# Modulation's second layer as three split products from the third tile on

## The reference

```python
ctx  = causal_ema(x, tau_ctx)
wg   = sigmoid(concat(x, ctx) @ Wg.T + bg)
gated = x * wg
h1   = gelu(x @ Wn1.T + bn1)                 # 128 channels
mod  = 0.5 + sigmoid(h1 @ Wn2.T + bn2)       # 4 numbers per token
traces = [causal_ema(gated * mod[..., d], tau[d]) for d in range(4)]
temporal = sum_d(traces[d] * softmax(blend)[d])
out  = (gelu(x @ Wsoma.T + bsoma) * sigmoid(temporal @ Wtemp.T + btemp)) @ Wout.T   # then a layer norm
```

## Time and profile before

| what | us |
|---|---|
| median of three runs | 1363.86 |
| profiled execution, its own time | 1364.18 |
| its span | 1362.5 |
| TensorE busy | 1353.7 |
| VectorE busy | 779.8 |
| ScalarE busy | 481.2 |
| GpSimd busy | 134.6 |

### The profile page before, as it was taken

The page is one execution under the profiler, slowest core; times in us unless marked ns, Lnnn a source line. Parts: engine busy times, 40 slices in busy tenths (PEclk is TensorE's granted clock), DMA queues, the critical chain, the costliest instruction groups (busy, mean ns, idle before and its releaser), DMA issues.

```text
span 1362.5 us, 15161 instructions
## 1 busy us (share of the span) xinstructions
PE 1353.7 (99%) x5912; PEld 1105.8 (81%) x5912; DVE 779.8 (57%) x1035; ACT 481.2 (35%) x799; POOL 134.6 (10%) x170
## 2 busy tenths in 40 slices
PE   9999999999999999999999999999999999999998
PEld 7888888888888888888887887878787878787877
DVE  4335243333252332342221586999999989898994
ACT  5444233332242432332321223243424342424253
POOL 5000100000100000100000221012101220032000
PEclk9999999999999999999999999999999999999999
DMA  5523433502532412631322945621232123212101
GB/s 134 140 70 116 125 107 123 155 16 101 139 121 80 154 43 87 165 109 46 101 78 86 210 158 193 163 89 62 93 124 94 62 94 124 93 63 93 47 16 62
DMA packets 68375, 140.89 MB, mean 103 GB/s; under 512 B 7328, under 2 KB 19616, under 8 KB 64336
## 3 DMA queue, kind: packets, MB, share of 16 engines
q1 hardware_dynamic: 61360, 116.71, 27.8%
q0 software_dynamic: 6944, 23.23, 5.7%
HBM read 86.85 MB, written 53.05 MB: 103 GB/s over the span
## 4 chain that ended last, share of the span: by engine, by line
PE 93%; DVE 4%; DMA 1%; issue 1%; ACT 0%; POOL 0%; SPq 0%; DVEq 0%; POOLq 0%
PE bank L990 31%; PE bank L991 31%; PE bank L992 31%; DVE drive L1423 1%; DMA x_slot<-x2hl_dram 1%; DVE drive L1408 1%; PE bank L1057 1%; DVE temporal L1433 0%; PE bank L1165 0%; DVE temporal L1423 0%; DMA mod_t<-mod_dram 0%; DMA x_raw<-in_x 0%; DVE spikes_lo L1267 0%; ACT temporal L840 0%; DVE gated L1392 0%
## 5 line engine op out<-in xcount | busy, mean ns | idle before, releaser
L1267 DVE TENSOR_TENSOR h_hl<-bank,h_hl 128x512 fp32r<-128x512 f32 x128 | 88.7, 693 | 465.9 <-ACT h_hl L862 465.9
L990 PE MATMUL bank<-x_hl,wa 128*128 128x512 f32 x512 | 199.7, 390 | 0.9 <-DVE x_hl L1267 0.9
L992 PE MATMUL bank<-x_hl,wa 128*128 128x512 f32 x512 | 199.2, 389 | 0.0
L991 PE MATMUL bank<-x_hl,wa 128*128 128x512 f32 x512 | 199.2, 389 | 0.0
L992 PE MATMUL bank<-h_hl,wa 128*128 128x512 f32 x512 | 199.2, 389 | 0.0
L990 PE MATMUL bank<-h_hl,wa 128*128 128x512 f32 x512 | 199.2, 389 | 0.0
L991 PE MATMUL bank<-h_hl,wa 128*128 128x512 f32 x512 | 199.2, 389 | 0.0
L858 ACT ACTIVATE bank<-bank,small_sb 128x512 f32<-128x512 f32 x128 | 84.2, 658 | 212.2 <-PE bank L992 212.1
L862 ACT ACTIVATE h_hl<-bank 128x512 fp32r<-128x512 f32 x128 | 76.7, 599 | 228.5 <-PE bank L992 228.0
L990 PEld LDWEIGHTS bank<-x_hl,wa 128*128 128x128 f32 x512 | 96.1, 188 | 23.1 <-DVE x_hl L1267 1.7
L992 PEld LDWEIGHTS bank<-x_hl,wa 128*128 128x128 f32 x512 | 96.2, 188 | 20.0
(11 more groups left out here) (163 smaller groups left out, 2315.9 us busy)
## 6 DMA issues: line engine op xcount, KB each, us to landing
x_slot<-x2hl_dram SPq DMA_DIRECT2D x32, 513.0 KB, 4.7
x2hl_dram<-x_hl POOLq DMA_DIRECT2D x28, 512.0 KB, 9.1
stage<-in_l_w SPq DMA_DIRECT2D x32, 256.0 KB, 3.1
x_dram<-x_raw SPq DMA_DIRECT2D x8, 1024.0 KB, 5.6
xt<-x_dram SPq DMA_DIRECT2D x8, 1024.0 KB, 5.7
mod_t<-mod_dram POOLq DMA_DIRECT2D x8, 1024.0 KB, 5.0
x_raw<-in_x SPq DMA_DIRECT2D x7, 1024.0 KB, 9.3
out<-y_sb SPq DMA_DIRECT2D x28, 256.0 KB, 2.3
```

Source lines behind the costliest of these rows:

```text
L990: eng.matmul(ps, w_hi, x_hi, start=first, stop=False)
L991: eng.matmul(ps, w_hi, x_lo, start=False, stop=False)
L992: return eng.matmul(ps, w_lo, x_hi, start=False, stop=final)
L1267: return eng.tensor_tensor(lo, raw, hi.bitcast(F32), ALU.subtract)
```

## The change

`mo(i)` for i > 1 becomes a `split_product` with 128x128 weights: the 4 columns of wn2 are put, high and low part, into a block of zeros `wn2_hl`. `h1` is split into `h1_hi` (ScalarE, at the place of `sumsq`) and `h1_lo` (VectorE, in place of `h1`). `mo(i)` is issued after 12 matmuls of `gate(i, 0)` and not after 6. On ScalarE `temporal_hi(r-1, 3)` goes ahead of `h1_of(r)`. On VectorE `h1_low(r)` is the first step of round r, behind `temporal_low(r-1, 2)`. `mo(0)` and `mo(1)` stay.

```diff
+        h1_lo = place("h1_lo", 4, [TOK], F32R)
+        h1_hi = place("h1_hi", 30, [TOK], F32R)
+        wn2_hl = place("wn2_hl", 127, [2, P], F32R)
# GpSimd
             for i in range(NT):
                 if i % HALVES == 0:
                     last_columns(i)
+                if i == 0:
+                    on.wait_ge(s_fc2, UNITS)
+                    eng.memset(wn2_hl[:, :, :].bitcast(F32), 0.0).then_inc(s_wn2, 1)
                 if i + 1 < NT:
                     modulation(i + 1)
# ScalarE
+            def h1_hi_of(i):
+                on.wait_ge(s_h1, i + 1)
+                on.wait_ge(s_pe["SS"], i - 1)
+                eng.activation(h1_hi[:, :], h1[:, :], ACT.Copy).then_inc(s_h1hi, 1)
# in o_of(i, m), m == 0, i > 0
                         on.wait_ge(s_pe["SS"], i)
+                        on.wait_ge(s_pe["MO"], min(i + 2, NT))
# ahead of soma_of(1, 0)
+            on.wait_ge(s_wn2, 1)
+            eng.activation(wn2_hl[:, 0, 0:TAUS], wn2_sb, ACT.Copy).then_inc(s_wn2, 1)
             for r in range(2, NT):
+                temporal_hi(r - 1, 3)
                 h1_of(r)
-                temporal_hi(r - 1, 3)
+                h1_hi_of(r)
                 mod_of(r)
# TensorE
             def mo(i):
+                if i > 1:
+                    on.wait_ge(s_wn2, 3)
+                    on.wait_ge(s_h1hi, i - 1)
+                    on.wait_ge(s_h1lo, i - 1)
+                    split_product(mo_bank(i)[:, :], wn2_hl[:, 0, :], wn2_hl[:, 1, :], h1_hi[:, :], h1_lo[:, :],
+                                  True, True).then_inc(s_pe["MO"], 1)
+                    return
# in gate(i, m)
-                    if m == 0 and c == 0 and i > 1:
+                    if m == 0 and c == 1 and i > 1:
                         mo(i)
# VectorE
+            def h1_low(i):
+                on.wait_ge(s_h1hi, i - 1)
+                low_part(h1_lo[:, :], h1[:, :], h1_hi[:, :]).then_inc(s_h1lo, 1)
             traces_d(1, 3)
+            on.wait_ge(s_wn2, 2)
+            low_part(wn2_hl[:, 1, 0:TAUS], wn2_sb, wn2_hl[:, 0, 0:TAUS]).then_inc(s_wn2, 1)
             temporal_low(1, 0)
             temporal_low(1, 2)
             for r in range(2, NT):
+                h1_low(r)
                 rows_rstd(r - 2)
```

More of the change, by code:

```diff
@@ L191, in build @@
         s_h1 = sem("s_h1")
+        s_h1hi = sem("s_h1hi")
+        s_h1lo = sem("s_h1lo")
+        s_wn2 = sem("s_wn2")
         s_soma = sem("s_soma")
```

## The result

The changed kernel takes 1370.46 us (median of 6 runs, 1369.61 to 1372.23), beside 1364.69 for the kernel before on the same chip (6 runs, 1363.69 to 1366.13). The ratio is 1.0044, with a 95% interval of 1.0033 to 1.0054: 6 us slower. Forecast was 1368.4, in a range of 1366.4 to 1372.2.

What follows compares the result with a forecast made beforehand. TensorE was taken to bound the kernel, VectorE close behind. Tile 2 +5.4, tiles 3 to 6 -1.8, tail +1.1, less 0.2 for mod_t, gave +4.5 us: 1363.86 to 1368.4, range 1366.4 to 1372.2.

Steps and rivals of the forecast that it cites:

- one gap in `gate(2, 0)`: Tile 2: TensorE stands 6.1 us near 893 in the middle of the gate, until VectorE's h1_lo is ready.
- ScalarE's move and VectorE's place as one chain: Tile 2: ts_hi, h1, h1_hi on ScalarE, then VectorE's h1_low to 899.05, so `mo(2)` starts at 899.2.
- te(1, 0): Behind tile 2's gate: starts at 902.7 where it started at 897.30, +5.4 us, carried on in full.
- rival (a): Clock falls in tile 2's stall; some 2.4 us more, at most about 3.5, giving 1370.8 us; chance 0.26.
- the full clock assumed behind the stall: Tile 2 behind the gap: matmuls 0.23 us apart, as no row shows a fall; the forecast's chance 0.50.
- The product's saving: `mo` in tiles 2 to 7: three split matmuls cost 0.69 us against 1.14 for fp32, saving 0.45 a tile.
- rival (b): h1_lo late in every tile, each waiting 0.3 to 0.5 us and losing its saving; 1370.0 us, chance 0.10.
- The tail's +1.1: Tile 7: later `mo(7)` delays mod_t, VectorE's drive and te(7, 0) by 1.1 us; ends 0.4 and 1.3.
- my 0.2 off for mod_t: Tail: 0.2 us taken off the +4.7 sum for the load of mod_t, giving +4.5.
- rival d: Tile 2's stall is mostly absorbed later by waits TensorE would have had anyway; about 1364 to 1366, chance 0.09.
- rival c: No stall in tile 2, if h1_lo(2) were ready by 893.1; 1361.2 us, chance 0.05.
- the offset between profile and median: Whole kernel: the median of runs taken 0.3 us below the profiled execution, so 1368.7 becomes 1368.4.

Runs made afterwards that it cites:

- e1: Changed kernel, but tile 2 keeps the plain fp32 product and the old ScalarE and VectorE order; 1364.55 us against 1365.21 before, ratio 0.9994.
- e4: Kernel before with one edit, no split: ScalarE does temporal_hi(r-1, 3) ahead of h1_of(r); 1373.37 us against 1365.21, ratio 1.0062.
- e5: Changed kernel with ScalarE's order undone in tile 2, VectorE's order kept; 1372.66 us against 1365.42 before, ratio 1.0052.
- e3: Changed kernel plus 25 matmuls, results unused, ahead of mo(2)'s waits to fill the gap; ratio 1.0028 against the kernel before.
- e8: Changed kernel with only tiles 3 to 6 split, plus 9 unused matmuls ahead of te(7, 0); 1363.74 us against 1365.96 before, ratio 0.9979.
- e7: e1 plus 9 matmuls, results unused, ahead of te(7, 0); 1365.07 us against 1365.96 for the kernel before, ratio 0.9993.
- e9: e1 measured once more, without filling, beside e7 and e8; 1365.38 us against 1365.96 for the kernel before, ratio 0.9994.

## Why the prediction was right, and where it was short

- **The direction and the place** were right: one gap in `gate(2, 0)`, ended by h_lo, 6.06 us for the 6.1 forecast. e1 (gone without tile 2) and e4 and e5 (each order alone makes it) show it. The text took ScalarE's move and VectorE's place as one chain; the runs showed that they are two causes, each enough.
- **te(1, 0)** was forecast 5.4 us later, and came 7.8 us later in step with the gate. The missing 2.4 us are rival (a), at the price it had been given (2.4), and e3 takes them off; in e5's profile they are 2.8. The step that failed is the full clock assumed behind the stall: the forecast priced the second layer and the twelve gate matmuls at 0.23 us a step, where all but the last of them started 0.43 apart. I held the fall less likely (0.26) than full clock (0.50), since no row showed one. So the time came where rival (a) had put it, 1370.8 for the 1370.46 measured; the range of the forecast alone, 1367.0 to 1369.7, missed it, and the stated range holds it because it took in most of this rival. The Trainium skill's rule on idle gaps ("TensorE: Matmul & The Clock Gate", section "HAM oscillation — how this bites in real kernels") was the better guide; the runs agree with it, with 0.50 of the clock behind 6.06 us of idle. The falls in the tail, behind idles of 2.0 us, are not what that section describes; for these only the runs here speak.
- **The product's saving** of 0.45 a tile came as 0.48: from the gate's start to the te behind it 6.17 to 6.19 us in tiles 3 to 7, where it was 6.65 to 6.68. None of it was lost to h_lo; rival (b) is out. From te(1, 0) to gate 7 the changed kernel's profile kept 1.27 of 1.9 us, beside a wait for x_slot loads ahead of `n1` of tile 7 (0.73 us more than a step, where there was none before); e5 and e3, with the same code there, kept 1.80 and 1.92, so the missing part belongs to the execution.
- **The tail's +1.1** came as +1.02 in the changed kernel; my 0.2 off for mod_t was not seen. The load of mod_t did get shorter, by more than that (5.0 us to land, for 6.8), but GpSimd waited 3.14 us for the store of `mod_row` ahead of it, for 1.53, and the two nearly cancel.
- **Nothing absorbed the stall** (rival d): behind te(1, 0) the stream was dense. That h_lo would be early (rival c) is out by 898.73.
- In sum, for the profiled executions: +7.8 - 1.3 + 1.0 = +7.5, from which 0.4 go off that the two differ by ahead of tile 2, against 7.1 in the spans. The medians differ by only 5.8, since the profiled execution of the kernel before lies 0.5 below the median of its six (1364.18 against 1364.69) and that of the changed kernel 0.9 above (1371.34 against 1370.46). I took the offset between profile and median as fixed, and it is not. Falls of the clock in the tail can be part of it; that they are was not shown.

## What to carry to other kernels

A change that saves work on the bounding engine by handing new work to the one close behind it must be checked at the tile where that one is latest, not at the common tile: here five tiles became 0.48 us shorter each, the last of them to no use, and the one with VectorE's queue full lost 7.8. When two queues were reordered together, undo both before judging either. And price a stall of TensorE with the clock behind it: here 2.4 us behind a stall of 6.1. Where an idle can't be avoided, matmuls without use into a free bank can keep the clock; they did in e3 behind `mo(2)` and in all 11 executions of e8, and not in 3 of the 11 of e7, where another idle was left unfilled.

## What the runs showed of the hardware that was not expected

- Short idles can be enough for a fall, and it does not come each time. In the profiles of e1, e3, e5 and e9 idles of 1.7 to 2.0 us ahead of ss(6) and 2.0 us ahead of te(7, 0), some 11 us apart, were followed by seven steps of 0.43 us; the changed kernel's profile passed idles of 1.9 and 2.0 us there at full clock.
- The fall in the tail did not come in the idle: the steps of 0.43 us began only after TensorE had started one matmul of te(7, 0) in e3 and e5, four in e1 and five in e9. In the stall of tile 2 the low level was there from the first matmul on (the changed kernel, e4, e5).
- Under the lower clock the plain fp32 product of 128x4 weights took 1.87 us for 1.02 (e4), and a split matmul started every 0.43 us for 0.23.
- A low part of 128x4 took 0.16 us on VectorE, with 0.08 between its start and the next one's; a full 128x512 took 0.69.
